# Attention scores and values of a windowed cross attention on four 32x32 parts of the matmul array

## The chip, the cores and the metric

The kernel runs on one core of a Trainium2 chip. The metric is device time in microseconds (us) of one execution, from three timed runs; a profiled execution beside them gives the trace. Engines are named as in the profile: PE (TensorE, matmuls) with PEld (its weight loads), DVE (VectorE), ACT (ScalarE), POOL (GpSimd) and SP (SyncE, which issues the DMAs).

## What is computed

Thirty-two batches of 128 x 1024 (channels x time). A layernorm of x feeds q, the context feeds k and v, each by a 128 x 128 projection. Eight heads of 16 channels attend over a sliding window of 16 positions. The result goes through a fourth projection onto x. Then a second layernorm, a gate over 8 experts of rank 64 of which the best two are used, and the sum onto x again.

```python
q = Wq @ layernorm(x) + bq;  k = Wk @ ctx + bk;  v = Wv @ ctx + bv    # 128 x 1024 each
dots = einsum('bhdt,bhdtw->bhtw', q, window(k)) * 16 ** -0.5          # w: 16 positions, t-8 .. t+7
out  = einsum('bhtw,bhdtw->bhdt', softmax(dots), window(v))
x = x + Wo @ out + bo
probs = softmax(layernorm(x) @ gate_w.T);  weights, sel = top_k(probs, 2);  weights /= weights.sum()
x = x + sum over e of w_full[:, e] * (layernorm(x) @ lora_A[e].T @ lora_B[e].T)
```

## The kernel before

One batch is one step of a software pipeline: in a step the engines work on five batches at once, called later, ahead, cur, prev and old (two ahead of cur to two behind it). The order of every engine is written out by hand in a function `step` (PE from L395, ACT from L534, DVE from L751, POOL from L870, SP from L257), and semaphores join them. Some steps are written out, the middle ones run in a loop of two steps.

Projections and the two expert products (`down`, 1024 to 520 columns, and `up`, 512 to 1024) are split into a high and a low part and run as three passes each, all from one helper (L318). A projection has six passes of 512 columns, `down` 48 passes of 264 or 256, `up` 24 of 512.

Attention works on query tiles of 16 positions with 32 keys each, 64 tiles in 4 chunks of 16. For the scores q is laid out block-diagonally by 8 DMAs per half (`place_q`, L231), so that one matmul on a 64 x 64 part of the array (L350) does four heads of a tile; two parts do the eight heads. A mask matmul opens each chunk (`open_scores`, L336). DVE takes the row maximum (L708), subtracts it (L714), ACT takes the exponential (L532), DVE sums (L722) and inverts (L726), POOL multiplies (L867), DVE transposes in 32 x 32 blocks (L733). For the values, v is transposed (L741) and laid out block-diagonally by 4 DMAs (`place_v`, L241), and one matmul on the whole array (L363) serves three tiles with one block of 32 keys; the rows of probabilities have gaps of 16 columns for that, so that a chunk is 768 columns. Even heads are copied out of the result by ACT (L527), odd heads joined by DVE (L658).

On PE the score groups (`scores_group`, L344) and value groups (`weighted_group`, L357) are dealt out in quarters of a chunk between the passes of the projections, `down`, `up` and the transposes (L373). k, the laid out q and the attention output exist once, so that the next batch's writer waits for this batch's last reader; the projected q and the normalised x of the second layernorm share one buffer, `q_xn2`. The attention output is split into high and low part in `mid_split` (L803, L887), the buffer in which `down` has its input.

Of the kernel before, what the change touches and what calls it, by code (L numbers as in the profile page):

```python
# [29 lines left out]
F32 = mybir.dt.float32  # L30
# [7 lines left out]
P = 128  # L38
# [6 lines left out]
QT = 16  # L45
# [5 lines left out]
HT = TILES // 2  # L51
GROUPS = 4
# [3 lines left out]
STRIDE = KT + QT  # L56
PC = CT * STRIDE
PAIRS = 4
HALVES = 2
HALF_P = P // HALVES  # L60
# [39 lines left out]
def build(nc, x, ctx, wqkvo, biases, down_w, up_w, ident_in, masks_in, consts_in, out):  # L100
    with ExitStack() as stack:
# [19 lines left out]
        q_diag = sb("q_diag", [P, 2, HT, HALF_P])  # L121
        v_diag = sb("v_diag", [P, PAIRS * PW * BLOCKS])
# [4 lines left out]
        q_xn2 = sb("q_xn2", [P, T])  # L127
        k_sb = sb("k_sb", [P, KPAD])
        v_sb = sb("v_sb", [P, VPAD])
        v_t = sb("v_t", [P, PW * BLOCKS])  # L130
        prob = sb("prob", [P, 2 * PC])
        prob_t = sb("prob_t", [P, CHUNKS * PC])
        attn = sb("attn", [P, T])
# [30 lines left out]
        q_diag_zero, v_diag_zero = sem("q_diag_zero"), sem("v_diag_zero")  # L164
# [3 lines left out]
        q_placed = [sem("q_placed0"), sem("q_placed1")]  # L168
        v_placed = sem("v_placed")
# [7 lines left out]
        prob_zero = sem("prob_zero")  # L177
# [18 lines left out]
        pieces = (piece(wqkvo, attn, 0, w_split, 0, 4 * P),  # L196
                  piece(down_w, prob_t, 2 * DW, down_split, 0, 3 * DW),
                  piece(up_w, v_diag, 0, up_split, 0, EK * T),
# [3 lines left out]
        def weights_of(m):  # L202

            return prob[:, m % 2 * PC:(m % 2 + 1) * PC].rearrange("p (n j) -> p n j", j=STRIDE)[:, :, 0:KT]
# [21 lines left out]
        def _(sp):  # L226
# [4 lines left out]
            def place_q(half):  # L231

                w = QT * HT
                for h in range(HEADS):
                    rows = slice(HD * h, HD * (h + 1))
                    at = HD * h % HALF_P
                    sp.dma_start(q_diag[rows, half, :, at:at + QT],  # L237
                                 q_xn2[rows, half * w:(half + 1) * w].rearrange(
                                     "p (n i) -> p n i", i=QT)).then_inc(q_placed[half], 16)

            def place_v():  # L241

                blocks = v_diag[:].rearrange("p (n c) -> p n c", c=P)
                for g in range(PAIRS):
                    rows = slice(PW * g, PW * (g + 1))
                    sp.dma_start(blocks[rows, :, PW * g:PW * (g + 1)],  # L246
                                 v_t[rows, :].rearrange("p (n c) -> p n c", c=PW)).then_inc(v_placed, 16)
# [9 lines left out]
            def step(later, ahead, cur, prev, old):  # L257
# [15 lines left out]
                if cur:  # L273
                    if cur.c >= 1:
                        sp.wait_ge(pv_done, cur.count(CHUNKS, 0))
                    else:
                        sp.wait_ge(v_diag_zero, 1)
                    sp.wait_ge(v_t_done, cur.count(1, 1))
                    place_v()
# [9 lines left out]
                if ahead:  # L289
                    if ahead.c >= 1:  # L290
                        sp.wait_ge(scores_done, ahead.count(CHUNKS, -2))
                    else:
                        sp.wait_ge(q_diag_zero, 1)
                    sp.wait_ge(q_out, ahead.count(1, 1))
                    place_q(0)
                    if ahead.c >= 1:
                        sp.wait_ge(scores_done, ahead.count(CHUNKS, 0))
                    place_q(1)
# [11 lines left out]
        def _(pe):  # L310
            pe.wait_ge(weights_lo, 1)
            pe.wait_ge(masks_ready, 2)
            pe.wait_ge(pads_zero, 5)
# [18 lines left out]
            def tiles(m, s):  # L332

                return [(t, m % 2 * CT + t) for t in range(s * CT // GROUPS, (s + 1) * CT // GROUPS)]

# [6 lines left out]


            def scores_group(m, s):  # L344

                for t, n in tiles(m, s):
                    at = (m * CT + t) * QT
                    for z in range(HALVES):
                        rows = slice(z * HALF_P, (z + 1) * HALF_P)
                        last = nc.tensor.matmul(bank_b[m % 2][rows, t * KT:(t + 1) * KT],  # L350
                                                q_diag[rows, m // 2, n, :],
                                                k_sb[rows, at:at + KT], start=False,
                                                stop=t == CT - 1, skip_group_check=True)
                if s == GROUPS - 1:
                    last.then_inc(scores_done, 1)

            def weighted_group(m, s):  # L357

                for i in ((0, 1, 2), (3, 4), (5, 6), (7, 8))[s]:
                    lo, hi = max(2 * i - 1, 0), min(2 * i + 2, CT)  # L360
                    at = m * PC + 2 * i * STRIDE - (2 * i - lo) * KT
                    n = m * CT // 2 + i
                    last = nc.tensor.matmul(bank_b[2 + m % 2][:, lo * PW:hi * PW],  # L363
                                            v_diag[:, n * P:(n + 1) * P],
                                            prob_t[:, at:at + (hi - lo) * KT],
                                            start=i == 0, stop=i == CT // 2, skip_group_check=True)
                if s == GROUPS - 1:
                    last.then_inc(pv_done, 1)
# [582 lines left out]
```

## Time and profile before

| | |
|---|---|
| median of three runs | 1298.94 us (1298.57 to 1300.41) |
| the profiled execution | 1300.73 us |
| its span, first to last instruction | 1298.8 us |
| PE busy | 1225.5 us, 94% |
| DVE busy | 891.5 us, 69% |
| POOL, ACT busy | 416.1 us, 380.5 us |
| granted TensorE clock, mean | 0.995 |

Busy time is the time in which at least one instruction of the engine runs. The end of a matmul in the trace is modelled, and matmuls overlap, so what one costs in a stream is read from starts. An f32 matmul of the program stands in the trace as two loads and two matmuls, an f32r one (the passes) as one of each.

### The profile page before, as it was taken

What the parts mean: (1) busy time and instruction counts of PE and PEld (TensorE: products, weight loads), DVE (VectorE), ACT (ScalarE), POOL (GpSimd) and SP (SyncE); (2) the same over time, 40 slices, a digit from 0 to 9 for tenths busy, and PEclk for the clock granted to TensorE, in tenths of its full rate; (3) what the DMA queues carried; (4) which work ended last, traced back from release to release, by engine and by line L of the source; (5) the groups of instructions that cost most, each with busy time, mean ns of one, the idle gap of its engine ahead of it and who ended that gap; (6) DMA issues with size and microseconds to landing.
All of it is one profiled execution on the core that took longest, in us unless ns stands there. A gap on an engine that the chain in (4) does not pass through costs nothing.

```text
span 1298.8 us, 34642 instructions
## 1 busy us (share of the span) xinstructions
PE 1225.5 (94%) x13953; PEld 1064.8 (82%) x14080; DVE 891.5 (69%) x2021; ACT 380.5 (29%) x553; POOL 416.1 (32%) x300
## 2 busy tenths in 40 slices
PE   3889999999999999999999999999999999999986
PEld 2778888888888888888888888888888888888875
DVE  3777667766767766767766767776767766767653
ACT  3332232322232322232322232322232322232211
POOL 3443333323333332332323333322332322333110
PEclk9989999999999999999999999999999999999999
DMA  6443433343443343443343443243443343443210
GB/s 214 79 88 67 99 91 75 83 90 62 97 91 81 77 97 64 88 93 75 81 95 60 95 92 88 70 99 67 83 93 87 70 99 64 85 93 76 58 40 33
DMA packets 427427, 108.44 MB, mean 83 GB/s; under 512 B 410001, under 2 KB 410129, under 8 KB 427153
## 3 DMA queue, kind: packets, MB, share of 16 engines
q1 hardware_dynamic: 427280, 106.13, 37.6%
q8 instruction: 136, 2.23, 0.7%
q14 instruction: 11, 0.08, 0.0%
HBM read 55.22 MB, written 16.78 MB: 55 GB/s over the span
## 4 chain that ended last, share of the span: by engine, by line
PE 91%; issue 3%; DVE 1%; DMA 1%; POOL 1%; SPq 1%; ACT 0%; POOLq 0%; DVEq 0%
PE bank_a L318 30%; PE bank_b L350 22%; PE bank_b L363 19%; PE bank_c L318 16%; PE bank_a L373 4%; DMA v_diag<-v_t 1%; POOL src_split L873 0%; SPq L237 0%; SPq L246 0%; POOL v_diag L878 0%; DMA ident<-ident_in 0%; DMA raw<-ctx 0%; DVE mid_split L767 0%; DMA q_diag<-q_xn 0%; POOL src_split L883 0%
## 5 line engine op out<-in xcount | busy, mean ns | idle before, releaser
L350 PE MATMUL bank_b<-k_sb,q_diag 64*64 64x32 f32 x8192 | 312.5, 222 | 31.2 <-issue 30.9
L350 PEld LDWEIGHTS bank_b<-k_sb,q_diag 64*64 64x64 f32 x8192 | 271.0, 136 | 83.9 <-issue 71.7
L363 PEld LDWEIGHTS bank_b<-prob_t,v_diag 128*128 128x128 f32 x2304 | 315.7, 192 | 23.8 <-DMA v_diag<-v_t 4.9
L363 PE MATMUL bank_b<-prob_t,v_diag 128*128 128x96 f32 (+2 forms) x2304 | 326.9, 270 | 4.6 <-DMA v_diag<-v_t 4.6
L318 PE MATMUL bank_a<-down_split,mid_split 128*128 128x264 f32 (+1 forms) x1536 | 267.5, 298 | 2.7 <-DVE mid_split L767 2.7
L867 POOL TENSOR_TENSOR prob<-prob,row_inv 128x512 f32<-128x512 f32 x128 | 146.4, 1144 | 323.4 <-DVE row_inv L726 323.4
L318 PE MATMUL bank_c<-src_split,w_split 128*128 128x512 f32 x576 | 221.1, 459 | 18.0 <-POOL src_split L873 14.2
L318 PEld LDWEIGHTS bank_a<-down_split,mid_split 128*128 128x128 f32 x1536 | 214.9, 189 | 15.9 <-ACT mid_split L548 3.0
L318 PE MATMUL bank_a<-up_split,ht_split 128*128 128x512 f32 x768 | 216.3, 405 | 4.0 <-DVE ht_split L808 3.6
L318 PEld LDWEIGHTS bank_a<-up_split,ht_split 128*128 128x128 f32 x768 | 138.2, 189 | 33.8 <-ACT ht_split L585 4.2
L733 DVE STREAM_TRANSPOSE prob_t<-prob 128x768 f32<-128x768 f32 x128 | 124.6, 973 | 30.4 <-POOL prob L867 30.4
L887 POOL TENSOR_TENSOR mid_split<-attn,mid_split 128x1024 fp32r<-128x1024 f32 x32 | 75.6, 2362 | 216.1 <-DVE mid_split L803 216.1
L873 POOL TENSOR_TENSOR src_split<-raw,src_split 128x1024 fp32r<-128x1024 f32 x32 | 75.6, 2361 | 170.3 <-DVE src_split L758 170.3
L532 ACT ACTIVATE prob<-prob 128x512 f32<-128x512 f32 x128 | 80.3, 627 | 164.0 <-DVE prob L714 163.8
L318 PEld LDWEIGHTS bank_c<-src_split,w_split 128*128 128x128 f32 x576 | 98.4, 197 | 28.3 <-issue 18.8
L606 ACT ACTIVATE q_xn<-resid_pair,shift,rstd 128x1024 f32<-128x1024 f32 x32 | 39.7, 1242 | 215.4 <-DVE shift L649 208.4
L585 ACT ACTIVATE ht_split<-bank_a 128x512 fp32r<-128x512 f32 x32 | 19.2, 600 | 282.7 <-PE bank_a L373 282.7
L714 DVE TENSOR_TENSOR prob<-bank_b,row_max 128x512 f32<-128x512 f32 x128 | 88.6, 692 | 5.6
L722 DVE TENSOR_REDUCE row_sum<-prob 128x16 f32<-128x512 f32 x128 | 84.6, 661 | 8.2 <-ACT prob L532 8.2
L697 DVE TENSOR_TENSOR h_sb<-bank_a,pick 128x256 f32<-128x256 f32 x64 | 27.1, 425 | 86.4 <-PE bank_a L318 84.1
L708 DVE TENSOR_REDUCE row_max<-bank_b 128x16 f32<-128x512 f32 x128 | 84.6, 661 | 2.5 <-PE bank_b L350 2.5
L527 ACT ACTIVATE attn<-bank_b,consts 128x256 f32<-128x256 f32 x128 | 59.2, 463 | 64.4 <-PE bank_b L363 64.4
(68 smaller groups left out, 1087.1 us busy)
## 6 DMA issues: line engine op xcount, KB each, us to landing
v_diag<-v_t SPq DMA_DIRECT2D x128, 132.0 KB, 3.8
raw<-x SPq DMA_DIRECT2D x32, 512.0 KB, 5.9
raw<-ctx SPq DMA_DIRECT2D x32, 512.0 KB, 3.4
q_diag<-q_xn SPq DMA_DIRECT2D x512, 32.0 KB, 2.4
resid_pair<-x SPq DMA_DIRECT2D x32, 512.0 KB, 3.4
out<-resid_pair SPq DMA_DIRECT2D x32, 512.0 KB, 2.6
v_diag<-up_w SPq DMA_DIRECT2D x1, 2048.0 KB, 9.3
prob_t<-down_w SPq DMA_DIRECT2D x1, 780.0 KB, 4.8
```

The costliest lines, as they stand in the source:

```text
L318: return nc.tensor.matmul(dst, st[:, s, st_cols], mv[:, m, mv_cols], start=start and n == 0, stop=stop and n == 2)
L350: last = nc.tensor.matmul(bank_b[m % 2][rows, t * KT:(t + 1) * KT], q_diag[rows, m // 2, n, :], k_sb[rows, at:at + KT], start=False, stop= ...
L363: last = nc.tensor.matmul(bank_b[2 + m % 2][:, lo * PW:hi * PW], v_diag[:, n * P:(n + 1) * P], prob_t[:, at:at + (hi - lo) * KT], start=i ...
L527: nc.scalar.activation(dst.rearrange("p (n i) -> p n i", i=QT), src[:, :, 0, :], ACT.Copy, scale=consts[:, 0:1]).then_inc(even_out, 1)
L532: nc.scalar.activation(weights_of(m), weights_of(m), ACT.Exp).then_inc(exp_done, 1)
L708: nc.vector.tensor_reduce(row_max[:, cols], scores, AX_X, ALU.max).then_inc(max_done, 1)
L714: nc.vector.tensor_tensor(weights_of(m), scores, row_max[:, cols].unsqueeze(2).broadcast_to([P, CT, KT]), ALU.subtract).then_inc(shifted, 1)
L722: nc.vector.tensor_reduce(row_sum[:, cols], weights_of(m), AX_X, ALU.add).then_inc(sum_done, 1)
L733: nc.vector.transpose(prob_t[:, m * PC:(m + 1) * PC], prob[:, m % 2 * PC:(m % 2 + 1) * PC]).then_inc(prob_t_done, 1)
L867: nc.gpsimd.tensor_tensor(weights_of(m), weights_of(m), row_inv[:, cols].unsqueeze(2).broadcast_to([P, CT, KT]), ALU.mult).then_inc(prob_d ...
L873: nc.gpsimd.tensor_tensor(src_split[:, 1, :], raw[:], src_split[:, 0, :].bitcast(F32), ALU.subtract).then_inc(xn_lo, 1)
L887: nc.gpsimd.tensor_tensor(mid_split[:, 1, :], attn[:], mid_split[:, 0, :].bitcast(F32), ALU.subtract).then_inc(attn_lo, 1)
```

## The change

Scores: q is laid out block-diagonally in 32 columns instead of 64, and each tile has four matmuls on the parts (0,0), (32,32), (64,64), (96,96) of the array, two heads each. Values: for each tile four matmuls on the same parts; a tile's 32 keys are one block of v transposed in blocks of 32 for even tiles, and for odd tiles a block of a copy that is shifted by 16 keys, which 8 DMAs make (`place_v`). The probabilities lose their gaps (512 columns per chunk). On PE the quarters are gone: a chunk of scores and a chunk of values stand together (`attend`), and projections, `down` and `up` are whole stages between them. k, the laid out q, v and the attention output have two buffers each; the attention output has its own split, `attn_split`, and `q_xn2` becomes `q_sb` and `xn2`. The orders of ACT, DVE, POOL and SP are rewritten to fit: the output projection comes before the second half of `down`, the k projection after the fourth chunk of scores, the q layout ahead of the x load.

```diff
-        q_diag = sb("q_diag", [P, 2, HT, HALF_P])
-        v_diag = sb("v_diag", [P, PAIRS * PW * BLOCKS])
+        q_diag = sb("q_diag", [P, 2, TILES, PW])
+        v_keys = sb("v_keys", [P, 4 * VPAD])
+        v_even = [v_keys[:, 2 * n * VPAD:(2 * n + 1) * VPAD] for n in range(2)]
+        v_odd = [v_keys[:, (2 * n + 1) * VPAD:(2 * n + 2) * VPAD - KT] for n in range(2)]
...
+                    sp.dma_start(odd[low, :], source[high, 0:T]).then_inc(v_placed, 16)
+                    sp.dma_start(odd[high, :], source[low, KT:KT + T]).then_inc(v_placed, 16)
...
-                    for z in range(HALVES):
-                        rows = slice(z * HALF_P, (z + 1) * HALF_P)
+            def scores_chunk(cur, m):
+
+                keys = k_sb[cur.parity]
+                for t in range(CT):
+                    n = m * CT + t
+                    for g in range(PAIRS):
+                        rows = slice(PW * g, PW * (g + 1))
                         last = nc.tensor.matmul(bank_b[m % 2][rows, t * KT:(t + 1) * KT],
...
+            def weighted_chunk(b, m):
+
+                for t in range(CT):
+                    n = m * CT + t
+                    values = (v_even, v_odd)[n % 2][b.parity][:, n // 2 * PW:(n // 2 + 1) * PW]
+                    at = n * PW
+                    for g in range(PAIRS):
+                        rows = slice(PW * g, PW * (g + 1))
+                        last = nc.tensor.matmul(bank_b[2 + m % 2][rows, t * PW:(t + 1) * PW],
+                                                values[rows], prob_t[rows, at:at + PW],
+                                                start=t == 0, stop=t == CT - 1, skip_group_check=True)
+                last.then_inc(pv_done, 1)
...
-                nc.vector.transpose(prob_t[:, m * PC:(m + 1) * PC],
-                                    prob[:, m % 2 * PC:(m % 2 + 1) * PC]).then_inc(prob_t_done, 1)
+                nc.vector.transpose(prob_t[:, m * CW:(m + 1) * CW],
+                                    prob[:, m % 2 * CW:(m % 2 + 1) * CW]).then_inc(prob_t_done, 1)
```

The order of PE before, in a step of the loop, from the first chunk of scores of cur to the first values of prev (a number behind x counts matmuls as written):

```order
L340 MATMUL bank_b<-mask_cols,mask_rows 128x512
L350 MATMUL bank_b<-k_sb,q_diag 64x32 x8
L318 MATMUL bank_c<-src_split,w_split 128x512 x2
L350 MATMUL bank_b<-k_sb,q_diag 64x32 x8
L318 MATMUL bank_c<-src_split,w_split 128x512 x2
L350 MATMUL bank_b<-k_sb,q_diag 64x32 x8
L318 MATMUL bank_c<-src_split,w_split 128x512
L350 MATMUL bank_b<-k_sb,q_diag 64x32 x8
L318 MATMUL bank_c<-src_split,w_split 128x512
L340 MATMUL bank_b<-mask_cols,mask_rows 128x512
L350 MATMUL bank_b<-k_sb,q_diag 64x32 x8
L373 MATMUL bank_a<-ident,q_xn 128x128 x4
```

The order of PE in the changed kernel, a step of the part behind the loop, from the v projection of cur to the q projection of ahead:

```order
L306 MATMUL bank_c<-src_split,w_split 128x512 x6
L324 MATMUL bank_b<-mask_cols,mask_rows 128x512
L334 MATMUL bank_b<-k_sb,q_diag 32x32 x64
L355 MATMUL bank_b<-prob_t,v_keys 32x32 x64
L363 MATMUL bank_a<-ident,xn 128x128 x8
L324 MATMUL bank_b<-mask_cols,mask_rows 128x512
L334 MATMUL bank_b<-k_sb,q_diag 32x32 x64
L355 MATMUL bank_b<-prob_t,v_keys 32x32 x64
L306 MATMUL bank_c<-src_split,w_split 128x512 x6
```

The v projection stood in two and one passes between quarters of scores; now it is one stage ahead of them, and a whole chunk of scores is followed by a whole chunk of the previous batch's values.

The order of DVE before, in the loop, from the second weighing of the experts' rank columns (`h_sb`) on:

```order
L697 TENSOR_TENSOR h_sb<-bank_a,pick 128x256
L803 CAST mid_split<-attn 128x1024
L707 REGISTER_ALU
L708 TENSOR_REDUCE row_max<-bank_b 128x16
L714 TENSOR_TENSOR prob<-bank_b,row_max 128x16x32
L808 TENSOR_TENSOR ht_split<-bank_a,ht_split 128x512
```

The order of DVE in the changed kernel, behind the loop, from the first of the two weighings to the split of `ht`:

```order
L635 TENSOR_TENSOR h_sb<-bank_a,pick 128x256
L646 TENSOR_REDUCE row_max<-bank_b 128x16
L652 TENSOR_TENSOR prob<-bank_b,row_max 128x512
L741 SCALAR_TENSOR_TENSOR resid_pair<-bank_c,bias,resid_pair 128x512 x2
L575 BN_STATS stats<-resid_pair 128x6 x2
L570 MEMSET fences 128x1
L579 BN_AGGR moments<-stats 128x2
L582 TENSOR_SCALAR var_eps<-moments 128x1
L660 TENSOR_REDUCE row_sum<-prob 128x16
L664 RECIPROCAL row_inv<-row_sum 128x16
L635 TENSOR_TENSOR h_sb<-bank_a,pick 128x256
```

The second weighing stood ahead of the third chunk's maximum; now it stands behind that maximum, x1, its statistics and the third row sum.

## Rows read from the trace of the kernel before

**Rows 1.** The page: busy us (share of the span) xinstructions, and the chain by engine.

```profile
PE 1225.5 (94%) x13953; PEld 1064.8 (82%) x14080; DVE 891.5 (69%) x2021; ACT 380.5 (29%) x553; POOL 416.1 (32%) x300
...
PE 91%; issue 3%; DVE 1%; DMA 1%; POOL 1%; SPq 1%; ACT 0%; POOLq 0%; DVEq 0%
```

**Rows 2.** Timeline of POOL: start us, us, engine line op names, xcount [idle before].

```profile
599.05 2.36 POOL L873 TENSOR_TENSOR src_split<-raw,src_split 128x1024 fp32r<-128x1024 f32 x1 [5.94 <-DVE src_split L758]
603.22 1.05 POOL L867 TENSOR_TENSOR prob<-prob,row_inv 128x512 f32<-128x512 f32 x1 [1.81 <-DVE row_inv L726]
...
637.68 2.36 POOL L873 TENSOR_TENSOR src_split<-raw,src_split 128x1024 fp32r<-128x1024 f32 x1 [5.18 <-DVE src_split L758]
```

**Rows 3.** Windows of one step and of an early low clock, columns named in the first line.

```profile
core 0: us, PE busy (x) PEld busy (x) DVE busy (x) ACT busy (x) POOL busy (x), PEclk, DMA share, GB/s
...
600.00:638.63 38.63, 37.96 (x444) 33.04 (x444) 27.56 (x64) 11.66 (x18) 12.74 (x10) 1.00 0.38 76
...
73.70:77.11 3.41, 1.57 (x54) 1.45 (x50) 3.00 (x5) 0.31 (x1) 2.78 (x2) 1.00 0.98 136
77.11:80.52 3.41, 2.62 (x9) 2.42 (x10) 2.99 (x5) 0.32 (x1) 1.80 (x2) 0.50 0.77 165
80.52:83.93 3.41, 3.41 (x14) 3.02 (x14) 0.07 (x1) 0.93 (x1) 0.00 (x0) 0.50 0.39 48
```

**Rows 4.** Timeline of PE; the number behind x counts records.

```profile
610.57 0.66 PE L350 MATMUL bank_b<-k_sb,q_diag 64*64 64x32 f32 x16 [0.16 <-issue]
611.16 0.98 PE L318 MATMUL bank_a<-down_split,mid_split 128*128 128x256 f32 x6
612.07 0.66 PE L350 MATMUL bank_b<-k_sb,q_diag 64*64 64x32 f32 x16
...
616.75 2.06 PE L350 MATMUL bank_b<-k_sb,q_diag 64*64 64x32 f32 x64 [0.16 <-issue]
618.74 0.91 PE L363 MATMUL bank_b<-prob_t,v_diag 128*128 128x64 f32 x6
```

**Rows 5.** Timeline of PE at the end of the kernel, where stages stand alone.

```profile
1277.84 1.07 PE L373 MATMUL bank_a<-ident,q_xn 128*128 128x128 f32 x8 [1.26 <-ACT q_xn L606]
1280.58 6.00 PE L318 MATMUL bank_a<-down_split,mid_split 128*128 128x264 f32 x48 [1.67 <-DVE mid_split L767]
...
1289.26 5.75 PE L318 MATMUL bank_a<-up_split,ht_split 128*128 128x512 f32 x24 [1.50 <-DVE ht_split L808]
```

**Rows 6.** Timeline of loads running in windows ending at 616.76, 616.82 and 616.87.

```profile
616.75 0.14 PEld L350 LDWEIGHTS bank_b<-k_sb,q_diag 64*64 64x64 f32 x2 [0.23 <-issue]
...
616.75 0.19 PEld L350 LDWEIGHTS bank_b<-k_sb,q_diag 64*64 64x64 f32 x4 [0.23 <-issue]
...
616.75 0.25 PEld L350 LDWEIGHTS bank_b<-k_sb,q_diag 64*64 64x64 f32 x6 [0.23 <-issue]
```

**Rows 7.** Timeline of loads in the longest stretch of value matmuls.

```profile
54.02 2.87 PEld L363 LDWEIGHTS bank_b<-prob_t,v_diag 128*128 128x128 f32 x25
```

**Rows 8.** The page's costliest groups: xcount | busy us, mean ns | idle before, releaser.

```profile
L350 PEld LDWEIGHTS bank_b<-k_sb,q_diag 64*64 64x64 f32 x8192 | 271.0, 136 | 83.9 <-issue 71.7
L363 PEld LDWEIGHTS bank_b<-prob_t,v_diag 128*128 128x128 f32 x2304 | 315.7, 192 | 23.8 <-DMA v_diag<-v_t 4.9
...
L733 DVE STREAM_TRANSPOSE prob_t<-prob 128x768 f32<-128x768 f32 x128 | 124.6, 973 | 30.4 <-POOL prob L867 30.4
L887 POOL TENSOR_TENSOR mid_split<-attn,mid_split 128x1024 fp32r<-128x1024 f32 x32 | 75.6, 2362 | 216.1 <-DVE mid_split L803 216.1
```

**Rows 9.** Timeline of PE near the start of the kernel.

```profile
36.98 3.63 PE L350 MATMUL bank_b<-k_sb,q_diag 64*64 64x32 f32 x64 [0.38 <-issue]
40.54 2.76 PE L318 MATMUL bank_c<-src_split,w_split 128*128 128x512 f32 x6
```

**Rows 10.** Window of the gate chain, columns as in rows 3.

```profile
610.45:613.02 2.57, 2.45 (x41) 2.23 (x42) 1.92 (x14) 0.23 (x2) 0.73 (x1) 1.00 0.42 59
```

**Rows 11.** Timeline of SP: issues of one step.

```profile
601.58 0.33 SPq L269 DMA_DIRECT2D raw<-ctx  x1
610.00 4.17 SPq L246 DMA_DIRECT2D v_diag<-v_t  x4
...
615.37 12.81 SPq L237 DMA_DIRECT2D q_diag<-q_xn  x16
```

**Rows 12.** The page's queue (packets, MB, share) and issue (KB, us to landing) of DMAs.

```profile
q8 instruction: 136, 2.23, 0.7%
...
raw<-x SPq DMA_DIRECT2D x32, 512.0 KB, 5.9
raw<-ctx SPq DMA_DIRECT2D x32, 512.0 KB, 3.4
```

More of the change, by code:

```diff
@@ L357, in weighted_group @@
[L357 to L368, printed above, removed]
+                last.then_inc(scores_done, 1)
@@ new lines, in step @@
+                    for n in range(6):
+                        last = project_pass(n, bank_c, 2, src_split)
+                    last.then_inc(v_done, 1)
+                attend(0, prev, 2)
+                if old:
+                    pe.wait_ge(xn2_done, old.count(1, 1))
+                    if old.c >= 1:
+                        pe.wait_ge(result_done, old.count(2, 0))
+                    transposes(bank_a, xn2, range(0, 4)).then_inc(xt_done, 1)
+                    transposes(bank_a, xn2, range(4, FK)).then_inc(xt_done, 1)
@@ new lines, in step @@
+                attend(1, prev, 3)
+                if ahead:
+                    pe.wait_ge(xn_hi, ahead.count(1, 1))
+                    pe.wait_ge(xn_lo, ahead.count(1, 1))
+                    if cur:
+                        pe.wait_ge(v_out, cur.count(1, 1))
+                    for n in range(6):
+                        last = project_pass(n, bank_c, 0, src_split)
+                    last.then_inc(q_done, 1)
+                if old:
+                    pe.wait_ge(xt_hi, old.count(2, 2))
+                    pe.wait_ge(xt_lo, old.count(2, 2))
+                    if old.c == 0:
+                        pe.wait_ge(weights_lo, 5)
+                    for f in range(FK):
+                        down(0, f)
@@ new lines, in step @@
+                if old:
+                    for f in range(FK):
+                        down(1, f)
+                attend(3, cur, 1)
+                if old:
+                    pe.wait_ge(h_done, old.count(2, 2))
+                    transposes(bank_a, h_sb, range(EK)).then_inc(ht_done, 1)
+                if ahead:
+                    pe.wait_ge(ctx_hi, ahead.count(1, 1))
+                    pe.wait_ge(ctx_lo, ahead.count(1, 1))
+                    if prev:
+                        pe.wait_ge(x1_done, prev.count(2, 2))
+                    else:
+                        pe.wait_ge(q_out, ahead.count(1, 1))
+                    for n in range(6):
+                        last = project_pass(n, bank_c, 1, src_split)
+                    last.then_inc(k_done, 1)
@@ L503, in _ @@
+                if old:
+                    pe.wait_ge(ht_hi, old.count(1, 1))
+                    pe.wait_ge(ht_lo, old.count(1, 1))
+                    for n in range(2):
+                        for e in range(EK):
+                            up(n, e)
             steps(pe, step)
@@ L828, in step @@
                     layernorm_stats(1, x1, ln2_step, prev)
[L829 to L832 removed]
+                if cur:
+                    weights_sum(cur, 2)
+                if old:
+                    weigh_experts(old, 1)
                 if prev:
```

357 lines of the change are left out of this document (117 added, 240 removed).

## Prediction, made before the changed kernel ran

> **What bounds the kernel now.** I read the page first: TensorE is busy 94% of the span and carries 91% of the chain that ended last, with VectorE at 69% [rows 1]. Then one step of the loop, cut out of the middle by windows: a step handles one batch and repeats every 38.63 us (POOL's split of x starts at 599.05 and 637.68 [rows 2]), in which PE is busy 37.96 and VectorE 27.56 [rows 3]. So the span is 32 x 38.63 = 1236.2 plus 62.6 for filling and emptying the pipeline. PE is the bound, and VectorE, with 11 us free per step, is the next one.
>
> **What a small matmul costs now.** Each f32 matmul as written leaves two records in the trace, a load and a matmul each (8192 for the 4096 score matmuls). In a long stretch 64 score records take 1.99 us (616.75 to 618.74), and 16 take 0.59 [rows 4]: (1.99 - 0.59) / 48 = 29.2 ns per record, and 0.12 us for leaving 64x64 parts. Six `down` passes before the next score group take 0.91 us, where at 0.119 each (first to second row of the end, 6.00 us for 48 less the last one's tail) they need 0.71 [rows 4, 5], so entering costs 0.20. One way in and out is 0.32.
>
> What are the 29.2 ns? This decides the case. Two 64-column loads start within 0.01 us, two more by 616.82, two more by 616.87 [rows 6]. Loads of 128 columns stand 2.87 / 25 = 0.115 us apart [rows 7], 0.9 ns per column, and a mean load of 128 columns is recorded with 192 ns where one of 64 has 136 [rows 8], again 0.9 ns per column. A 64-column load so takes some 0.057 us. Records only 0.029 us apart therefore mean that the loads of two parts run at the same time, one per row half. Near the start, where a pass of 512 columns too takes 0.46 us (2.76 / 6) instead of 0.24, 64 records take 3.56 us, 55.6 ns each [rows 9]; an instruction sequencer at a fixed rate would not slow down like this. So I take the price as one load per part, 0.9 ns x columns, with the parts side by side.
>
> **The change, part by part, per step.**
> (a) Scores become 256 matmuls on four 32x32 parts (before 128 on two 64x64), values 256 on four (before 36 of 128x128). Records: 512 + 512 = 1024, before 256 + 72. With 32 columns a load takes 0.029; four parts at once give a record every 7.3 ns, and with 2 to 3 ns lost per load (a part of 64 columns has one every 58.4 for 57) a round of four takes 31.7, 7.9 per record. 1024 x 7.9 = 8.1 us. Before: 256 x 0.0292 + 72 x 0.115 = 15.8. Gain on PE 7.7.
> (b) Whole stages: the score groups between projection, `down` and transposes made 12 entries into parts per step; now scores and values of a chunk follow each other in the same mode, 4 entries. 8 x 0.32 = 2.6 us off PE.
> (c) What stays on PE: 48 passes of 512 columns at 5.75 / 24 = 0.240, 48 `down` passes 6.00, 12 transposes at 1.07 / 8, four masks at about 0.24 [rows 5]: 11.5 + 6.0 + 1.6 + 1.0 = 20.1, with four entries 21.4. The same tariff gives the kernel before 20.1 + 3.8 + 15.8 = 39.7 against a measured 38.63, so I take off the 1.1 of overshoot: 20.3. PE now needs 20.3 + 8.1 = 28.4 us.
> (d) VectorE: the probability transpose shrinks from 768 to 512 columns, 0.97 to about 0.66 by length, four times: 27.56 - 1.24 = 26.3 [rows 3, 8].
> (e) Its waits. PE and VectorE are now within 2 us of each other, and VectorE's order decides. Walking one step from the end of the last `up` pass: the v projection (6 x 0.24) holds back the cast of x, and scores 0 come 0.2 + 0.24 + 0.20 + 1.02 + 0.2 later: about 0.9 idle. The transpose of chunk 1 now stands behind POOL's attention split: 2.36 + 1.05 against 1.5 of VectorE's own work, 2.0 idle; POOL's norm also holds the transposes of chunks 2 and 3, 0.4 and 1.0 [rows 2, 8]. The second `up` half ends 0.9 after VectorE is ready. The gate chain runs 2.57 us with 1.92 busy [rows 10], and signals between short dependent operations add about as much again: 1.3. Sum 26.3 + 0.9 + 2.0 + 0.4 + 1.0 + 0.9 + 1.3 = 32.8.
> (f) PE waits in return. The transposes of h now need the second `h_sb`, which VectorE issues behind x1, its statistics and the third row sum: 3 to 3.5 us in which PE has nothing, and 1 to 2 more for `ht_split`. Queued behind them are the k projection and `up`, for which VectorE waits at the end of the step. Early in the run a stretch of 3.41 us in which PE was busy for 1.57 was followed by two at a granted clock of 0.50, in the second of which PE was busy throughout [rows 3]. So gaps of this kind may bring the low level (1.2 instead of 2.4 GHz) every step. It costs at most half of 3.41 us where PE is late anyway, and nothing where it is early; I take 0.6, bounds 0 and 1.7.
> (g) Double buffers for k, q tiles, v and the attention output take waits away that did not end last before; I cost them at nothing, since PE had 0.67 us idle per step [rows 3].
> (h) The SP queue: v moves as 8 transfers of 16 whole rows. The 128-row load of ctx takes 0.33 to issue, so at most 2.6 us against 4.17 before; 8 q transfers of twice the pieces take 0.80 to 1.60 each, 6.4 to 12.8 us, against 12.81 for 16 [rows 11]. They stand ahead of the x load of the batch two on, which was in front of them. With q out 11 us into the step (PE's stages from v to q, 9.5, ScalarE's write 1.1), x is issued at 17 to 24 and lands 3.4 to 5.9 later [rows 12], at 21 to 30; VectorE asks for it at about 27. Cost 0, upper bound 2.6 us per step.
>
> Sum: 32.8 + 0.6 = 33.4 us per step, 62.6 + 32 x 33.4 = 1131. The profiled execution took 1300.73 (span 1298.8) and the median of the three runs is 1298.94, so span and median agree, and I give **1130 us**.
>
> **The rivals.**
> *Two parts at a time.* If the matmuls keep the order of the program, the second record of one part can overlap only the first of the next. That gives a record every 31.7 / 2 = 15.9 ns and PE needs 20.3 + 16.2 = 36.5: 62.6 + 32 x 36.5 = 1231. For it: loads come in twos, never more [rows 6]. Against it: the kernel before had only two parts to offer. A slower supply of instructions lands in the same place: the trace's 14,080 load records become 36,352, the 2.23 MB of the instruction queue [rows 12] some 4.6 MB, in bursts.
> *A record costs what it costs.* If 29.2 ns is a floor per record and not two loads side by side, the tiled part takes 1024 x 29.2 = 29.9 and PE 50.2 us per step: 62.6 + 32 x 50.2 = 1669, slower by 370. It decides from 17.9 ns per record on, (38.63 - 20.3) / 1024. For it: no row shows a shorter mean. Against it: pairs that start together [rows 6], the slowdown with the clock [rows 9], and loads of 128 columns at 0.115.
> The Trainium skill, "TensorE: Matmul & The Clock Gate", section "Wait — 56ns, not 53.3ns?", says that starts of matmuls never come closer than about 25 ns however few the columns. By that rule the tiled part would take 1024 x 25 = 25.6 us and the kernel 62.6 + 32 x 45.9 = 1531, an estimate from that page; it is this rival at its mildest. The two loads within 0.01 us speak for starts closer than that between parts.
> *The clock.* If every step runs 3.4 us at 0.50 in VectorE's way, 34.5 us per step: 1167. This lies inside the forecast's range.
>
> **How the numbers follow.** Four parts side by side, VectorE the bound: 0.65, from 1080 (no clock loss, waits 1.1 smaller) to about 1170, or 1210 with x late. Two at a time or slow supply: 0.14, 1190 to 1290. Floor per record: 0.17, 1500 to 1700. The rest, 0.04, is near the old time. The range for 8 in 10 is 1080 to 1260. This kernel's measurement can tell about 0.2%. Faster 0.81, same 0.02, slower 0.17.
>
> **What would show it.** Right: score and value stretches of 256 records take about 2 us, the step is 32 to 34.5 us, VectorE is near 80% busy and PE clearly below its 98%, and PE waits for `h_sb` each step. (a) is wrong if 256 records take 4 us (two at a time) or 7.5 us (floor). (e) is wrong if VectorE is not the longest; (f) if PE's gap before the transposes of h is missing or the clock stays at 1.00; (h) if VectorE waits for x. If PE is still above 95% at a shorter step, the price per record was too low.

## The result, and the profile after

The changed kernel takes 1618.83 us (median of four runs, 1617.61 to 1635.21) against 1298.83 us in the same comparison: 1.249 times as long, 95% interval 1.241 to 1.257. The forecast was 1130 us, with a range of 1080 to 1260. Both the time and the sign were wrong.

The page of the changed kernel, with busy us (share of the span) xinstructions, the granted clock in tenths of full speed over 40 slices, the instruction queue (packets, MB, share) and the chain that ended last; these answer to [rows 1, 12]:

```profile
span 1616.9 us, 78855 instructions
...
PE 1209.3 (75%) x36352; PEld 1028.7 (64%) x36352; DVE 947.0 (59%) x2021; ACT 380.8 (24%) x553; POOL 411.2 (25%) x300
...
PEclk9678768888887887778878777797778778777888
...
q8 instruction: 311, 5.10, 1.3%
...
PE 73%; issue 23%; DVE 1%; SPq 1%; DMA 1%; ACT 1%; POOL 0%; POOLq 0%
```

"issue" is time in which the engine waited for nothing that the profile shows. It was 3% of the chain and is 23% now. The waits of PE say where (us in total, times, longest):

```profile
PE bank_b L355 <- issue: 289.0, 126, 3.1
PE bank_b L334 <- issue: 69.8, 51, 3.8
```

L355 is the value matmul and L334 the score matmul. One step as a window, which answers to the first window of [rows 3], and a stretch of it as PE's timeline (start us, us, x records, idle before), which answers to [rows 4]:

```profile
787.00:835.84 48.84, 36.22 (x1129) 31.39 (x1129) 27.90 (x61) 11.57 (x17) 12.74 (x9) 0.79 0.29 68
```

```profile
793.96 0.37 PE L334 MATMUL bank_b<-k_sb,q_diag 32*32 32x32 f32 x18
797.87 1.66 PE L334 MATMUL bank_b<-k_sb,q_diag 32*32 32x32 f32 x107 [3.54 <-issue]
799.30 0.24 PE L355 MATMUL bank_b<-prob_t,v_keys 32*32 32x32 f32 x1
799.33 0.25 PE L334 MATMUL bank_b<-k_sb,q_diag 32*32 32x32 f32 x3
799.35 0.45 PE L355 MATMUL bank_b<-prob_t,v_keys 32*32 32x32 f32 x17
801.34 1.71 PE L355 MATMUL bank_b<-prob_t,v_keys 32*32 32x32 f32 x110 [1.54 <-issue]
802.98 2.93 PE L306 MATMUL bank_c<-src_split,w_split 128*128 128x512 f32 x6
...
822.49 1.25 PE L334 MATMUL bank_b<-k_sb,q_diag 32*32 32x32 f32 x126
823.57 0.19 PE L355 MATMUL bank_b<-prob_t,v_keys 32*32 32x32 f32 x1
...
823.60 0.87 PE L355 MATMUL bank_b<-prob_t,v_keys 32*32 32x32 f32 x78
826.81 0.62 PE L355 MATMUL bank_b<-prob_t,v_keys 32*32 32x32 f32 x48 [2.34 <-issue]
```

Three things are to be seen. First, 126 records take 822.49 to 823.57, 8.6 ns each: the four parts do run side by side. Second, PE stops in the middle of a stretch, for 1.5 to 3.5 us, and between two stops stand 107 + 1 + 3 + 17 = 128 matmul records. With their 128 loads that is 256 instructions. The page has 78855 instructions of all engines on 311 packets of the instruction queue, 254 to a packet, and 5.10 MB on 311, 16.4 kB each. So PE stops at the border of a packet of 256 instructions. The packets' own times in the trace fit: one starts at 812.44, where PE stops at about 812.50, and one at 824.17, where PE stops at 824.47; PE goes on about 2.5 us behind each start. Third, the projection at 802.98 takes 2.93 us where it needs 1.64 at full clock: the granted clock is low (0.50 in the window from 797.10 to 807.20) behind the stops. Counted from 60 us on, PE's timeline has 168 idle stretches of over 0.7 us that sum to 361 us (half of them last 1.8 to 2.6 us), and the clock is at its low level for 634 us of the trace. In this document such idle stretches are called stops; the expectations below count them a little wider, 403 us for these 361.

The whole trace bears the border out. Between two neighbouring stops lies a number of PE instructions (matmuls, loads, waits) that is within 6 of a multiple of 256 in 144 of 167 cases, where chance would give about 8; and 159 of the 168 stops end 2.1 to 3.0 us behind the start of a packet of the instruction queue.

### The profile page after: what moved, and what is told of

Its sections match the earlier page's. It is cut to its first block, busy times and chain, and to the rows that moved or that the text cites. A ratio compares the mean times of both kernels' runs of the same rounds, so it can differ in the third digit from the quotient of the medians.

```text
span 1616.9 us, 78855 instructions
## 1 busy us (share of the span) xinstructions
PE 1209.3 (75%) x36352; PEld 1028.7 (64%) x36352; DVE 947.0 (59%) x2021; ACT 380.8 (24%) x553; POOL 411.2 (25%) x300
## 4 chain that ended last, share of the span: by engine, by line
PE 73%; issue 23%; DVE 1%; SPq 1%; DMA 1%; ACT 1%; POOL 0%; POOLq 0%
PE bank_a L306 25%; PE bank_c L306 17%; PE bank_b L355 13%; PE bank_b L334 12%; PE bank_a L363 5%; PE bank_b L324 2%; SPq L233 0%; DMA raw<-x 0%; DVE stats L575 0%; DMA ident<-ident_in 0%; ACT raw L550 0%; DMA v_keys<-v_keys 0%; POOL src_split L801 0%; SPq L243 0%; ACT k_sb L540 0%
## 5 line engine op out<-in xcount | busy, mean ns | idle before, releaser
L355 PE MATMUL bank_b<-prob_t,v_keys 32*32 32x32 f32 x16384 | 230.5, 209 | 289.0 <-issue 289.0
L355 PEld LDWEIGHTS bank_b<-prob_t,v_keys 32*32 32x32 f32 x16384 | 202.1, 120 | 305.1 <-issue 304.0
L334 PE MATMUL bank_b<-k_sb,q_diag 32*32 32x32 f32 x16384 | 202.9, 203 | 70.7 <-issue 69.8
L334 PEld LDWEIGHTS bank_b<-k_sb,q_diag 32*32 32x32 f32 x16384 | 179.4, 114 | 117.8 <-issue 116.3
L306 PEld LDWEIGHTS bank_c<-src_split,w_split 128*128 128x128 f32 x576 | 149.2, 273 | 61.7 <-issue 22.3
L807 POOL TENSOR_TENSOR attn_split<-attn_pair,attn_split 128x1024 fp32r<-128x1024 f32 x32 | 76.3, 2383 | 341.3 <-DVE attn_split L716 341.3
L671 DVE STREAM_TRANSPOSE prob_t<-prob 128x512 f32<-128x512 f32 x128 | 90.3, 706 | 69.3 <-POOL prob L795 69.3
L596 DVE SCALAR_TENSOR_TENSOR attn_pair<-bank_b,consts,attn_pair 128x256 f32<-128x256 f32 x128 | 60.1, 470 | 65.7 <-ACT attn_pair L485 65.7
L741 DVE SCALAR_TENSOR_TENSOR resid_pair<-bank_c,bias,resid_pair 128x512 f32<-128x512 f32 x64 | 47.9, 751 | 69.6 <-PE bank_c L306 69.3
L683 DVE TENSOR_TENSOR resid_pair<-bank_a,resid_pair 128x512 f32<-128x512 f32 x64 | 43.6, 681 | 74.7 <-PE bank_a L306 74.5
```

What stands on the lines that cost most here:

```text
L306: return nc.tensor.matmul(dst, st[:, s, st_cols], mv[:, m, mv_cols], start=start and n == 0, stop=stop and n == 2)
L355: last = nc.tensor.matmul(bank_b[2 + m % 2][rows, t * PW:(t + 1) * PW], values[rows], prob_t[rows, at:at + PW], start=t == 0, stop=t == CT ...
L596: nc.vector.scalar_tensor_tensor(dst, src[:, :, 1, :], consts[:, 1:2], dst, ALU.mult, ALU.add).then_inc(attn_done, 1)
L671: nc.vector.transpose(prob_t[:, m * CW:(m + 1) * CW], prob[:, m % 2 * CW:(m % 2 + 1) * CW]).then_inc(prob_t_done, 1)
L807: nc.gpsimd.tensor_tensor(attn_split[:, 1, :], attn[prev.parity], attn_split[:, 0, :].bitcast(F32), ALU.subtract).then_inc(attn_lo, 1)
```

## Experiments

Theory 1: what costs the time is the supply of instructions. They come in packets of 256, mostly 3.4 us or more apart, PE now uses one up in 1.1 us, and the low clock is a consequence of the stops. Rival: the small parts themselves are slow or lower the clock, or the shifted v, the buffers or VectorE's new order hold the step.

**The same matmuls, spread out.** e1_spread is the changed kernel with another order on PE: each chunk stands alone between two stages of passes.

```diff
-                attend(0, prev, 2)
-                transposes(...)
-                attend(1, prev, 3)
-                project q;  down(0, 0..7)
-                attend(2, cur, 0)
+                scores(0);  transposes(...);  values(prev, 2);  project q
+                scores(1);  down(0, 0..3);    values(prev, 3);  down(0, 4..7)
+                scores(2);  down(1, 0..3);    values(cur, 0)
...
```

> The changed kernel with its stages in another order on PE: each chunk of scores and each chunk of values stands alone, with the x transposes, the q or o projection or half of a down product between them, so that no more than 256 instructions of 32x32 parts follow each other instead of 512 or 1024. Same matmuls, same result. Theory 1 (the instruction supply in blocks of 256 instructions makes the idle times of 2.5 us, and these bring the low clock): the idle time called issue falls from 403 us to under 150, the mean clock rises from 0.805 to above 0.93, time 1150 to 1350 us. Rival 2 (the 32x32 matmuls themselves let the clock fall, whatever the gaps): the clock stays near 0.8 and the time above 1450. Rival 3 (a record on a 32x32 part has a fixed cost and the idle times are an artefact): time stays at 1600 to 1700, since four more entries into parts are added.

Measured: 1496.04 us, 1.1515 times before (1.1423 to 1.1607), outside the 1150 to 1350 us that theory 1 gave. The order alone gives back 123 us, the low clock falls from 634 to 297 us and the mean clock rises to 0.90, but the stops still sum to 275 us, against under 150 expected: theory 1 has the sign right and the size wrong. A chunk of 128 matmul records is, with its loads, a packet of its own, and at 2290 PE instructions a step almost nine packets have to come:

```profile
743.50 1.02 PE L334 MATMUL bank_b<-k_sb,q_diag 32*32 32x32 f32 x96
746.38 0.45 PE L334 MATMUL bank_b<-k_sb,q_diag 32*32 32x32 f32 x32 [1.85 <-issue]
746.76 1.68 PE L306 MATMUL bank_a<-down_split,mid_split 128*128 128x256 f32 x12
748.37 0.90 PE L355 MATMUL bank_b<-prob_t,v_keys 32*32 32x32 f32 x83
750.08 0.59 PE L355 MATMUL bank_b<-prob_t,v_keys 32*32 32x32 f32 x45 [0.80 <-issue]
```

From the stop ahead of 746.38 to the one ahead of 750.08 it is 32 + 12 + 83 = 127 records, again one packet but for a record.

**Half of the matmuls.** e2_two_parts is the changed kernel with two of the four parts left out, in scores and in values, so heads 4 to 7 are not computed; one matmul of 512 columns per values chunk fills the bank first (its lines are left out here).

```diff
-                    for g in range(PAIRS):
+                    for g in range(2):
```

> The changed kernel with scores and values computed on two of the four parts only (heads 4 to 7 are left out; a matmul of 512 columns fills the value banks first), so 512 records of 32x32 parts per step instead of 1024, in the same order. Theory 1: instructions per step fall from 2276 to some 1260, idle issue time falls to under 60 us, the clock rises to above 0.95, the time to 1110 to 1220 us with VectorE as the bound. Rival 2 (small parts let the clock fall): clock stays under 0.88 and the time above 1300. Rival 3 (fixed cost per record): PE saves 512 x 0.0085 = 4 us per step only, 1480 to 1500 us.

Measured, one run: 1215.12 us. The long waits for issue in scores and values are gone, 23 us are left in a projection; 67 idle stretches of over 0.7 us remain, 115 us in all, mostly for the shifted v (41 us) and for VectorE:

```profile
PE bank_b L346 <- DMA v_keys<-v_keys: 41.3, 21, 6.2
PE bank_a L306 <- DVE ht_split L761: 34.1, 29, 1.8
PE bank_c L306 <- issue: 22.9, 12, 2.8
```

The mean clock was 0.911, lower than the 0.95 expected: 218 us at the low level, 1.9 us per us of stops. The changed kernel has 1.8 and e8_waits, which has no small part, 1.5, so the idle stretches can account for it; that the small parts add nothing is argued, not shown.

The run shows one thing more. A step takes 35.6 us here, though the supply hardly stops PE and PE has 512 records (4.4 us) less to do. So even then the new schedule would have missed the forecast's 33.4 us: PE waits for the shifted v and for VectorE, and the low clock behind these waits costs up to 3.4 us a step (an estimate, half of 218 us over 32 steps).

**Whole stages alone.** e3_before_whole is the kernel before with whole chunks on PE instead of quarters; parts, buffers and VectorE's order are the old ones.

```diff
-                    for s in range(GROUPS):
-                        if cur:
-                            scores_group(m, s)
-                        if m == 2 and old:
-                            down(1, 2 * s)
-                            down(1, 2 * s + 1)
+                scores(2)
+                if old:
+                    for f in range(FK):
+                        down(1, f)
```

> The kernel before with part (b) of the change alone: the same matmuls on 64x64 parts and on the whole array, but whole chunks and whole products on PE instead of quarters, other engines unchanged. Theory 1 (switches cost 0.32 us each and nothing else stands against whole stages, bursts being 128 instructions): 8 switches less, up to 2.6 us per step, time 1215 to 1290 us, clock at 0.99, no idle issue time over 1 us. Rival (whole stages make PE wait for VectorE and POOL as much as they save): 1290 to 1340 us.

Measured: 1229.23 us, 0.9454 times before (0.939 to 0.9518). This is part (b) of the change and nothing else, and it is faster than both the kernel before and the changed one. Its step is 36.32 us, with PE busy for 35.95, so PE is still the bound:

```profile
600.00:636.32 36.32, 35.95 (x442) 32.21 (x441) 27.60 (x64) 11.49 (x19) 12.70 (x9) 1.00 0.40 89
```

**Scores on four parts alone, in the old quarters.** e4_before_scores4 changes the width of the laid out q and the loop over the parts.

```diff
-        q_diag = sb("q_diag", [P, 2, HT, HALF_P])
+        q_diag = sb("q_diag", [P, 2, HT, PW])
-                    for z in range(HALVES):
-                        rows = slice(z * HALF_P, (z + 1) * HALF_P)
+                    for z in range(PAIRS):
+                        rows = slice(z * PW, (z + 1) * PW)
```

> The kernel before with its scores alone on four 32x32 parts (q laid out in 32 columns), still dealt out in quarters between the passes, values on the whole array as before. Theory 1 (four parts run side by side at 8 to 11 ns per record, supply of instructions is enough when they are spread: 1136 + 512 = 1648 instructions per step): PE saves 256 x 0.0292 - 512 x 0.0095 = 2.6 us per step, time 1190 to 1260 us, clock above 0.97. Rival 2 or 3 (small parts cost clock or a fixed 29 ns per record): 1400 to 1540 us.

Measured: 1281.3 us, 0.9846 times before (0.9769 to 0.9924). The parts are worth 1.5%, less than expected (1190 to 1260 us): 32 stops (17 before) sum to 56 us, and the low clock holds for 94 us.

**Both together.** e5_whole_scores4 is e3_before_whole with the edit of e4_before_scores4.

> The kernel before with two parts of the change and no more: whole chunks and whole products on TensorE (as e3_before_whole, 1229 us), and the scores on four 32x32 parts (as e4_before_scores4); values, buffers and VectorE's order stay as before. A scores chunk is now 128 matmul records in one piece and stands alone between passes of 128-row tiles. Theory 1 (each part is worth its own price, what hurts is instructions that come faster than they are supplied): the scores save 64 x 29.2 - 128 x 7.9 ns = 0.86 us a chunk, 3.4 us a step, of which VectorE's own time leaves about 2; 1412 TensorE instructions in a step of 34 to 36 us are 5.5 blocks of 256 at over 6 us each, so gaps stay under 150 us in all. 1150 to 1240 us. Theory 2 (the small parts themselves cost the clock, whatever the supply): clock under 0.95, 1240 to 1330 us.

Measured: 1228.16 us, 0.944 times before (0.939 to 0.9491), the same as e3_before_whole. What the parts save in a chunk is given back at the packet borders, and where PE is earlier it waits for v_diag (16.1 us in all, 5.0 in e3_before_whole). One step has both kinds of chunk:

```profile
614.67 3.10 PE L318 MATMUL bank_a<-down_split,mid_split 128*128 128x256 f32 x24
617.93 1.29 PE L350 MATMUL bank_b<-k_sb,q_diag 32*32 32x32 f32 x128 [0.16 <-issue]
619.82 2.19 PE L363 MATMUL bank_b<-prob_t,v_diag 128*128 128x64 f32 x18 [0.60 <-DMA v_diag<-v_t]
...
633.96 1.12 PE L350 MATMUL bank_b<-k_sb,q_diag 32*32 32x32 f32 x108 [0.50 <-issue]
636.83 0.38 PE L350 MATMUL bank_b<-k_sb,q_diag 32*32 32x32 f32 x20 [1.75 <-issue]
```

The chunk at 617.93 needs 1.3 us where one of e3_before_whole needs 2.0; the one at 633.96, which meets a border, needs 3.2.

**As many instructions as the changed kernel, on old ground.** e6_scores4_twice is e5_whole_scores4 with every scores chunk computed twice; e7_scores2_twice is e3_before_whole with the same edit, on two 64x64 parts.

```diff
-                        open_scores(cur, m)
-                        for s in range(GROUPS):
-                            scores_group(m, s)
+                        for again in range(2):
+                            open_scores(cur, m, again)
+                            for s in range(GROUPS):
+                                scores_group(m, s, again)
```

> e5_whole_scores4 with each scores chunk computed twice, one right behind the other (the second opening clears the bank, so that the output stays the same): 1024 more TensorE instructions a step, 2440 in all, about as many as the changed kernel has (2290), but none of its values on parts, its shifted v or its buffers. Theory 1 (supply): the 4 blocks of 256 instructions more must come at 3.4 to 3.8 us each within the long chunks, so the step gets 9 to 14 us longer than in e5 and TensorE idles without a releaser for over 250 us in all: 1450 to 1700 us. Theory 2 (no limit but the array): 512 records x 7.9 ns and four openings are 5 us a step, 160 us in all: 1340 to 1400 us with issue idle as in e5.

> e3_before_whole with each scores chunk computed twice, on two 64x64 parts as before: 512 more TensorE instructions a step (1412 in all, as in e5), each record at 29.2 ns. Theory 1: 256 records of 29.2 ns are 7.5 us, with the openings 8.3 us a step, of which the slack of TensorE in e3 takes 2 to 4: 1370 to 1500 us, clock 0.97 or more, and issue idle of TensorE under 40 us, since 256 instructions at 14.6 ns take 3.7 us, which is no faster than the blocks came in the changed kernel. Theory 2 (it is the number of instructions in a step and not their rate): issue idle over 100 us.

Measured, one run each: 1839.04 us and 1511.55 us, both above the ranges of theory 1 (1450 to 1700 and 1370 to 1500). In e6_scores4_twice 512 more records of 8.6 ns, which are 5 us of work with the openings, lengthen the step from 36.9 to 55.9 us; I had expected 9 to 14 us more. The stops go from 64 to 295 us (7.2 us a step) and the low clock from 67 to 483 us, which at half speed costs up to 6.5 us a step (an estimate); together that is about the 19 us. There is no shifted v, no second buffer and no new order of VectorE in this kernel, and it stops like the changed one:

```profile
824.55 1.44 PE L350 MATMUL bank_b<-k_sb,q_diag 32*32 32x32 f32 x128 [0.16 <-issue]
826.24 0.52 PE L350 MATMUL bank_b<-k_sb,q_diag 32*32 32x32 f32 x36 [0.25 <-issue]
828.24 0.98 PE L350 MATMUL bank_b<-k_sb,q_diag 32*32 32x32 f32 x92 [1.48 <-issue]
```

In e7_scores2_twice 256 more records on 64x64 parts lengthen the step by 9.3 us (7.5 for the records at 29.2 ns, 1.2 for four openings). It has the 1412 PE instructions of a step that e5_whole_scores4 has, but PE is busy 93% of the span, the clock is 0.999, and no wait for issue is over 0.5 us (49 us in 223 short ones, where under 40 was expected; the kernel before has 31 in 125):

```profile
PE bank_b L350 <- issue: 49.4, 223, 0.5
```

So it is the rate within a burst, not the number of instructions in a step. At 29.2 ns a record 256 instructions last 3.7 us, and at 8.6 ns 1.1 us. Of the distances between the starts of neighbouring packets, from 200 us on, the closest twentieth are up to 3.4 us, the closest quarter up to 3.8 us and the median is 4.3 us in the changed kernel (279 packets), and 3.3, 3.8 and 4.4 us in e6_scores4_twice (296).

**Idle without small parts.** e8_waits is e3_before_whole with 128 waits behind each scores chunk, all on a value long reached.

```diff
+                        for _ in range(128):
+                            pe.wait_ge(pads_zero, 5)
```

> e3_before_whole with 128 waits put behind each scores chunk on TensorE's queue, all on a semaphore that is long past its value: 512 more instructions a step that do nothing on the array. Theory 1 (instructions arrive in blocks of 256 at 3.4 us or more, prefetched by one): besides the waits' own time (unknown, 5 to 60 ns each, 2.6 to 30 us a step) instruction fetches rise by 2 blocks a step, 64 in all, to about 200, and if a wait takes under 13 ns they show as stretches at the supply's rate. Theory 2: a wait that is already met costs nothing and is not fetched as an instruction of its own: the kernel stays at 1229 us with 136 fetches.

Measured, one run: 2343.49 us. A chunk's 128 waits take 6.4 us, 50 ns each, and stand in the trace as 64 instructions, so that 256 of them would last far longer than a packet's 3.4 us; the fetches rose by 32, not 64 (168 in all), which fits the 64. So waits are not free, as theory 2 had it, but theory 1 was not tested: this run says nothing on the supply. What it does show is the clock. It has no 32x32 part, PE idles 6.4 us four times a step, and the granted clock is at its low level for 1221 us, 0.74 in the mean:

```profile
828.36 5.04 PE L318 MATMUL bank_a<-down_split,mid_split 128*128 128x256 f32 x24 [6.34 <-issue]
833.56 2.06 PE L350 MATMUL bank_b<-k_sb,q_diag 64*64 64x32 f32 x64 [0.16 <-issue]
841.99 4.02 PE L363 MATMUL bank_b<-prob_t,v_diag 128*128 128x64 f32 x18 [6.37 <-issue]
```

24 passes of `down` take 5.04 us behind the idle time, where the same 24 take 3.10 in e5_whole_scores4. Idle time of PE on the issue side is enough to bring the low clock.

**The spread kernel with the scores on two parts.** e9_scores2_values4 is e1_spread with 64 columns in the laid out q and two 64x64 parts; values on four parts, shifted v, buffers and VectorE's order stay.

> e1_spread (1496 us) with the scores on two 64x64 parts instead of four 32x32: values on four parts, shifted v, double buffers and VectorE's order all stay. 512 TensorE instructions a step fewer (1780 instead of 2290, 7 blocks of 256 a step instead of 9), and the scores' bursts come at 14.6 ns an instruction instead of 4. Theory 1 (supply): TensorE's issue idle, 10.5 us a step in e1, halves or better (110 to 220 us in all), the clock goes from 0.90 to 0.94 or more, and the scores cost 4 x (64 x 29.2 - 128 x 8.6 ns) = 3.1 us a step more: 1496 - 170 - 60 + 100 = 1366, 1300 to 1430 us. Theory 2 (the shifted v, its DMAs or the doubled buffers hold the step, not the supply): the scores cost 3 us more a step and nothing is given back, 1480 us or more.

Measured: 1351.92 us, 1.0387 times before (1.0323 to 1.045). The expectation was 1366. Taking four-part scores out makes e1_spread 144 us faster, though PE's own work gets longer by 3 us a step (an estimate, 4 x (64 x 29.2 - 128 x 8.6) ns). The stops fall from 275 to 112 us and the clock rises to 0.941:

```profile
PE bank_b L355 <- issue: 68.3, 70, 2.7
PE bank_a L306 <- DVE ht_split L786: 29.7, 25, 3.2
...
PE bank_b L334 <- issue: 29.3, 140, 1.3
```

Side by side, the times as above and the rest from each profiled execution (stops are the idle stretches of over 0.7 us in PE's timeline, from 60 us on; the low clock is summed over the trace; PE instructions are matmuls, loads and waits):

| kernel | time us | step us | PE instructions a step | stops us | low clock us |
|---|---|---|---|---|---|
| before | 1298.8 | 38.6 | 896 | 22 | 16 |
| e3_before_whole | 1229.2 | 36.3 | 900 | 13 | 26 |
| e5_whole_scores4 | 1228.2 | 36.9 | 1408 | 64 | 67 |
| e4_before_scores4 | 1281.3 | 38.7 | 1412 | 56 | 94 |
| e7_scores2_twice | 1511.6 | 45.6 | 1412 | 9 | 6 |
| e9_scores2_values4 | 1351.9 | 40.0 | 1776 | 112 | 160 |
| e1_spread | 1496.0 | 44.4 | 2292 | 275 | 297 |
| changed kernel | 1618.8 | 48.8 | 2293 | 361 | 634 |
| e6_scores4_twice | 1839.0 | 55.9 | 2436 | 295 | 483 |

The supply theory stands: the kernels that stop are those with bursts on four parts, whatever the rest of them is, and they stop at the borders of packets (e6_scores4_twice in 144 of 161 distances, e1_spread in 157 of 188). No run changed the supply itself. How the packets are fetched (how many ahead, and what sets their distance, which fell to 1.9 us for single pairs in e5_whole_scores4) was not measured; that one is requested when another is used up fits the starts of the packets, and is argued, not shown.

## Why the prediction was wrong, step by step

**(a) The price of a record: nearly right in bursts, and applied where it doesn't hold.** Forecast 7.9 ns, measured 8.6 at full clock and 13.4 at the low one. "Two at a time" and "a record costs what it costs" are refuted as mechanisms. The Trainium skill, "TensorE: Matmul & The Clock Gate", section "Wait — 56ns, not 53.3ns?", has a floor of about 25 ns between starts of matmuls; on four parts the trace shows 8.6 ns. The step that failed is the next one: 1024 x 7.9 = 8.1 us per step presumes that 2048 instructions are there when PE wants them. I had the supply in view, as one sentence in the first rival ("a slower supply of instructions lands in the same place"), saw that the queue's 2.23 MB would double [rows 12], and gave it 15.9 ns per record and 1231 us without working out a rate. The rate needs one more look at the kernel before: of the distances between its packets of 256 instructions even the closest twentieth of 120 are 3.1 to 3.3 us, and a burst at 7.9 ns per record uses one up in 1.0. With 1024 records a step, which are eight packets, two of them in every `attend`, the stops were to be expected. They cost 12.6 us in the step shown below, and some 11.6 on average (361 us over about 31 steps).

**(f) The clock: idle time does lower it, but another idle time than the one I had, and far more of it.** I took 0.6 us a step, with a bound of 1.7, for one gap of PE in a step, the wait for `h_sb`. That gap is missing: PE waits 1.5 us for `h_sb` in the whole run. There are four or five stops instead, and the clock is low for 634 us. The step from 787.00 to 835.84 closes the account: its stops are 2.75 + 3.54 + 1.54 + 2.45 + 2.34 = 12.6 us, and PE is busy for the other 36.2. Three projections at the low clock take 2.9 instead of 1.64 us each and the two `down` stages 3.80 and 4.29 instead of 3.1, together 5.8 us too long. The bursts add about 1.8: some 240 records at the low clock (13 to 15 ns each instead of 8.6) 1.2 of it, and some 240 from 809.67 on, which have short pauses in them at full clock (11 ns each), 0.6. That leaves 28.6, where **(c)** and (a) had 28.4. So of the 15.4 us between 48.84 and the forecast 33.4, the price of the work was not the fault.

**(b) Whole stages: right.** Forecast 2.6 us a step, e3_before_whole shows 38.63 - 36.32 = 2.3.

**(d) VectorE: wrong by about 3 us a step, hidden here.** The probability transpose went to 706 ns, nearly as forecast (0.66). But VectorE's busy time did not fall by 1.2 us a step; it rose by 1.7, to 947.0 us from 891.5:

```profile
L723 DVE CAST src_split<-raw 128x1024 fp32r<-128x1024 f32 x32 | 60.2, 1883 | 11.4 <-DMA raw<-ctx 5.8 <-PE bank_c L306 5.5
...
L610 DVE CAST top_atf<-top_at 128x2 f32<-128x2 uint32 x32 | 27.8, 869 | 1.1
```

The same two casts took 684 and 176 ns before. In the new order they run beside POOL's splits: the cast at 806.02 takes 1.82 us while POOL works on this from 804.91 to 807.28:

```profile
804.91 2.37 POOL L807 TENSOR_TENSOR attn_split<-attn_pair,attn_split 128x1024 fp32r<-128x1024 f32 x1 [11.63 <-DVE attn_split L716]
```

That is 1.9 us a step which I had costed at nothing, since I had taken each duration from a row in which the two engines did not overlap so. The trace shows the hold directly: 30 of the 32 casts of L723 start while POOL's split L807 runs, and each of them ends 0.55 us behind the end of that split, however early it started (1.80 to 2.23 us long); the casts that no split overlaps take 0.63 to 0.70, in L723 as in L695 and L716. Who starts first matters: in the kernel before the same cast starts 0.16 us ahead of POOL's multiply of the probabilities and takes 0.69, and there the multiply takes 1.44 instead of 1.05. The Trainium skill, "GPSIMD Engine Reference", section "1. Specifications", says that GpSimd's path to the buffer memory is shared with VectorE, with contention when VectorE's instruction is in a two-port mode or has two SBUF inputs. The trace agrees as far as it goes: these two casts lengthened most, by 1.2 and 0.7 us, and a reduction hardly at all (669 ns for the row sums, before 661). That the overlap with the split stretches the cast is shown by the ends above; that a shared path is the reason is the page's word, and no run moved the split away from the cast.

**(e) and the forecast's bound.** VectorE was not the longest at any point of the changed kernel: it waits 126 us for scores and 75 for `up`. Whether 32.8 was right as VectorE's own limit can't be read from these runs, but what there is speaks for a higher one: e2_two_parts, with the same VectorE order and hardly a stop of the supply, has steps of 35.6 us, and e9_scores2_values4 has its quickest at 38.3 us, with PE waiting for `ht_split` 30 us in all.

**(g)** cost nothing visible: PE hardly waits for a buffer in the changed kernel. **(h)** x arrived in time (VectorE waits 2.6 us for it in all), though the v transfers take 0.6 us each to issue, 5 us for eight, not at most 2.6. In e2_two_parts, where the supply no longer holds PE back, PE waits 41 us for them (up to 6.2 at a time): a cost that the stops hide in the changed kernel.

**The chances.** The case with 0.65 had two halves, four parts side by side and VectorE the bound; the first came true, the second did not, and treating the first as the same as "faster" was the error. The time lies in the 1500 to 1700 us of the floor per record, but that is chance: the floor's mechanism is refuted by the 8.6 ns. Both rivals were about the array, and the one about the queue had been folded into the milder of them.

## What to carry to other kernels

Splitting a matmul into smaller parts multiplies instructions, and a price per matmul is valid only as long as the instruction queue keeps up: divide the instructions of the longest burst by the packet size, and compare with the closest spacing of the instruction packets in a trace (here 256 instructions per 3.4 us, 13 ns an instruction). If the burst is quicker, cost it at the queue's rate as an upper estimate (eight packets at 3.4 us are 27 us a step here; bursts and stops came to 8.8 + 12.6 = 21), and add the low clock that its stops bring. Of a change with several parts, the plain one (whole stages, fewer switches of tile shape) can be worth more alone than the whole: 1229 us against 1619.

## What the runs showed of the hardware that was not expected

- PE stops at multiples of 256 instructions, 0.8 to 3.8 us each and 2.2 in the median, in bursts that use 256 in 1.1 us; bursts that use 256 in 3.7 us (e7_scores2_twice) don't stop.
- Four 32x32 parts take a record every 8.6 ns at full clock, and every 13.4 ns at the low one.
- Stops of 1.5 to 3.5 us bring the granted clock to 0.5 though PE has work (634 us low in the changed kernel); idling alone does it too (1221 us low in e8_waits).
- A wait on a value long reached costs PE 50 ns (6.4 us for 128 in e8_waits).
- A cast of 128x1024 on VectorE that starts while POOL's split of 128x1024 runs ends 0.55 us behind the split, and so takes 1.8 to 2.2 instead of 0.7 us (30 casts); where the cast starts first, it is POOL's operation that gets longer (1.44 instead of 1.05 us).
